# A four-layer graph kernel: the second layer's masked sums with two rounded four-byte pieces of the features over the whole array width instead of three bf16 pieces on half widths

## The chip, the core and the metric

The kernel runs on one core of a Trainium2 chip. The metric is the time that the device takes for one execution, in microseconds (us); several executions are timed and their median is compared. A profile of one more execution shows what each engine did: TensorE (PE in the rows, PEld for its weight loads), VectorE (DVE), ScalarE (ACT), GpSimd (POOL) and SyncE (SP), which only issues transfers.

## What is computed

Four layers of a graph network over 4096 nodes with 64 features each follow one another, each with a residual sum and a normalization of the rows. All take the same adjacency matrix `adj` (4096 x 4096, about 1.6% of it not zero, plus the diagonal). The change touches the second layer alone. Cut to what matters there:

```python
A = adj - diag(diag(adj))
node_support = concat([(A > 0) @ h, (A < 0) @ h], axis=1)      # 0/1 masks times features
edge_output = gru_cell(node_support, h, ...)
hw = h @ W_gat
h_plus, h_minus = (A > 0) @ hw, (A < 0) @ hw
e_plus = leaky_relu(concat([h_plus, h_minus], axis=1) @ a)
e_minus = leaky_relu(concat([h_minus, h_plus], axis=1) @ a)
att = softmax(where(A > 0, e_plus, where(A < 0, e_minus, -9e15)), axis=1)
node_output = gru_cell((att * A) @ hw, h, ...)
out = diag(adj)[:, None] * (edge_output + node_output)         # then residual and row norm
```

Two kinds of products over all nodes are needed: the 0/1 masks times `h`, and the positive and negative values of `A` times `h`.

## The kernel before

The layers run as stages of one program, and each engine has a hand-written list of instructions; semaphores alone set the order between engines. The adjacency matrix does not fit on the chip and is loaded anew in every stage, in tiles of 512 rows by 1024 columns (2 MB).

The second layer works in four quarters `q` of 1024 columns each. A quarter has sixteen steps `m`, two for each tile; a step covers two blocks of 128 rows. The loop stands once on each engine's list (lines 917, 1446 and 2096), and a count of finished steps, `pair_used`, ties them together: masks and negative parts have two buffers each, so those of step `m` may be written once TensorE has ended step `m - 2`.

In a step:
- VectorE counts the edges of the upper half for a later layer (`extend_chain`, L2093, two calls), writes the two 0/1 masks `more` and `less` in bf16 (L2122 and L2124; L2117 and L2118 where the tile holds the quarter's own diagonal, which is first read and cut out, L2106 to L2113), and last the positive part in place (L2127). That one waits for ScalarE, which reads the same tile.
- ScalarE writes the negative part (L1453) and codes of the edge counts, which it stores (L1440, L1443).
- TensorE multiplies. Features are the weights and tiles stream. L947 and L948 multiply the four-byte features with the positive and the negative part; L953 and L955 multiply the masks with the features as three bf16 pieces `parts`, whose sum is the four-byte number. Each matmul has 64 weight columns; the positive side goes to the lower half of the array's columns, the negative side to the upper half, and the two run at the same time. PSUM banks 0 and 1 collect the first kind, 2 and 3 the second.

The pieces are made ahead of the loop: ScalarE casts (`split_act`, L1228) and VectorE subtracts (`split`, L1910), alternating, for four groups of eight row blocks.

Between the steps each engine's list has the rest of the layer, worked on one or two quarters late. For the quarter before: both engines copy the sums (`copy_sums`), TensorE makes the scores (step 2), VectorE the gate (steps 3, 5), TensorE spreads the shares (step 7), VectorE weighs (8), TensorE makes the eight `hidden` blocks (steps 10 and 11, in banks 5 to 7, read by ScalarE in `read_hidden`), and VectorE the gates (13 to 15). For the quarter before that: joining, row norm, and the product with the third layer's weights (`turn_rows`, `supports`, bank 4). Behind the loop the same follows for the last quarter, while the third layer's products (`decayed`) begin in between.

Memory around it: the loads of SyncE's queue go to a ring of four tiles (L583), each when the tile that held the slot is used up; the third layer's codes and the fourth's edges take the same room later (L593 to L601, L628).

## Time and profile before

| | |
|---|---|
| median of 3 runs | 1562.92 us (1557.15 to 1565.25) |
| the profiled execution: time, span of its instructions | 1558.08 us, 1556.3 us |
| busy over the span: TensorE, VectorE, ScalarE, GpSimd | 88%, 79%, 59%, 14% |
| TensorE's granted clock over the span | 0.951 of full speed |
| the second layer's stage, first to last product of its loop | 528.8 to 977.9 us |
| products L947, L948 (records, mean of one) | 512 each, 598 ns |
| products L953, L955 (records, mean of one) | 768 each, 380 ns |

The busy share of an engine is a mean over stages with different limits, so what a change in one stage is worth has to be read in that stage. Matmuls are pipelined: a record lasts from its first to its last column, and the distance between the starts of two records tells what one costs in a stream.

### The profile page before, as it was taken

The numbers are of one execution on the slowest core, as the hardware profiler recorded it, in microseconds if no ns is written. First come the engines' busy times: TensorE is split into PE (matmuls) and PEld (weight loads), VectorE is DVE, ScalarE is ACT, GpSimd is POOL, SyncE is SP. The second block draws the span as 40 slices with busy tenths as digits, with TensorE's granted clock in tenths as the row PEclk, the third lists the DMA queues.
The fourth block names the chain that finished last, engine by engine and source line by source line (L and its number), as shares of the span: only waits on it lengthen the run. The fifth ranks groups of instructions, "written<-read, shape, count | busy, mean of one in ns | idle before, by whom it ended". The sixth has DMA issues, their size and how long they took to land. (4 is left out here: it accounts for less than half of the span.)

```text
span 1556.3 us, 20315 instructions
## 1 busy us (share of the span) xinstructions
PE 1370.9 (88%) x7818; PEld 591.1 (38%) x7818; DVE 1228.1 (79%) x1617; ACT 922.3 (59%) x888; POOL 222.0 (14%) x148
## 2 busy tenths in 40 slices
PE   5999999779977699999999999979977988888970
PEld 1433333223322444444444444534423433333430
DVE  4899866766776877876986977448697898899977
ACT  0000187348743454545555556676788899999964
POOL 1000000000000000000000000134134444444430
PEclk9999999999999699999999999999978999999995
DMA  9999599979999255553543551134723646646600
GB/s 338 409 409 409 232 400 409 413 289 394 409 414 413 109 206 213 179 183 130 183 180 126 183 180 45 55 96 151 240 92 125 199 137 209 209 136 209 215 14 27
DMA packets 135895, 348.92 MB, mean 224 GB/s; under 512 B 7732, under 2 KB 57208, under 8 KB 135544
## 3 DMA queue, kind: packets, MB, share of 16 engines
q1 hardware_dynamic: 119968, 329.27, 57.3%
q10 hardware_dynamic: 15832, 18.36, 3.3%
q8 instruction: 62, 1.02, 0.3%
q14 instruction: 33, 0.27, 0.1%
HBM read 329.78 MB, written 17.83 MB: 223 GB/s over the span
## 5 line engine op out<-in xcount | busy, mean ns | idle before, releaser
L947 PE MATMUL ps<-ring,X 128*64 128x512 f32 x512 | 264.3, 598 | 15.2 <-DVE ring L2127 15.2
L948 PE MATMUL ps<-work,X 128*64 128x512 f32 x512 | 264.3, 598 | 0.0
L1453 ACT ACTIVATE work<-ring 128x2048 f32<-128x2048 f32 x64 | 122.3, 1911 | 156.9 <-PE ps L955 123.4
L953 PE MATMUL ps<-work 128*64 128x512 bf16 x768 | 208.3, 380 | 0.0
L955 PE MATMUL ps<-work 128*64 128x512 bf16 x768 | 208.3, 380 | 0.0
L719 POOL TENSOR_TENSOR ring<-ring,work 128x1024 f32<-128x1024 f32 x72 | 171.1, 2377 | 224.8 <-DVE work L2377 224.8
L816 PE MATMUL ps<-ring,work 128*64 128x512 f32 x672 | 158.1, 615 | 22.8 <-DMA ring<-in_adjT 22.7
L705 POOL TENSOR_SCALAR work<-ring 128x1024 int16<-128x1024 uint8 x24 | 27.7, 1156 | 1008.8 <-DMA ring<-codes 933.1
L953 PEld LDWEIGHTS ps<-work 128*64 128x64 bf16 x768 | 84.8, 110 | 177.9 <-issue 152.4
L1279 ACT ACTIVATE work<-work,code_bias 128x2048 uint8<-128x2048 bf16 (+1 forms) x32 | 62.3, 1947 | 92.0 <-DVE work L1870 82.0
L1214 ACT ACTIVATE turn_in<-ps 128x512 f32<-128x512 f32 x12 | 7.2, 597 | 180.8 <-PE ps L816 180.3
L1834 DVE TENSOR_TENSOR work<-work,ring 128x1024 f32<-128x1024 f32 (+1 forms) x103 | 102.2, 992 | 9.7 <-DMA ring<-in_adjT 8.0
L2127 DVE TENSOR_SCALAR ring<-ring 128x2048 f32<-128x2048 f32 x64 | 78.1, 1220 | 39.5 <-ACT work L1453 39.5
L1079 PE MATMUL ps<-work 64*128 64x512 f32 x288 | 88.1, 691 | 17.6 <-DVE work L2390 16.0
L816 PE MATMUL ps<-ring,X 128*64 128x512 f32 x352 | 85.7, 631 | 17.2 <-DMA ring<-in_adjT 17.2
L816 PE MATMUL ps<-work 128*64 128x512 f32 x352 | 83.3, 618 | 11.1 <-DMA work<-in_adjT 11.1
L816 PEld LDWEIGHTS ps<-ring,work 128*64 128x64 f32 x672 | 45.9, 140 | 122.3 <-issue 86.6
L947 PEld LDWEIGHTS ps<-ring,X 128*64 128x64 f32 x512 | 68.7, 137 | 58.5 <-issue 16.8
L2390 DVE SCALAR_TENSOR_TENSOR work<-ps,work 128x1024 f32<-128x1024 f32 x72 | 87.4, 1214 | 1.1 <-PE ps L1090 1.1
L2122 DVE TENSOR_SCALAR work<-ring 128x2048 bf16<-128x2048 f32 x48 | 58.7, 1224 | 35.7 <-PE ps L955 35.5
L2093 DVE SCALAR_TENSOR_TENSOR stage_words<-ring,stage_words 128x512 bf16<-128x512 f32 x124 | 84.9, 684 | 0.6
L955 PEld LDWEIGHTS ps<-work 128*64 128x64 bf16 x768 | 84.8, 110 | 0.0
(366 smaller groups left out, 2768.1 us busy)
## 6 DMA issues: line engine op xcount, KB each, us to landing
ring<-in_adjT SPq DMA_DIRECT2D x88, 2048.0 KB, 16.0
work<-in_adjT SPq DMA_DIRECT2D x28, 2048.0 KB, 19.7
ring<-in_adjT SPq DMA_DIRECT2D x24, 1024.0 KB, 9.3
ring<-in_adjT SPq DMA_DIRECT2D x48, 512.0 KB, 3.6
ring<-codes SPq DMA_DIRECT2D x32, 512.0 KB, 3.7
ring<-in_adjT SPq DMA_DIRECT2D x64, 256.0 KB, 3.0
codes<-work ACTq DMA_DIRECT2D x32, 256.0 KB, 6.1
codes<-work ACTq DMA_DIRECT2D x64, 128.0 KB, 1.7
```

What stands on the lines that cost most here:

```text
L719: nc.gpsimd.tensor_tensor(u.edges, u.edges, u.angle, ALU.mult).then_inc(weighted, 1)
L816: mm = nc.tensor.matmul(ps[i * F:(i + 1) * F, a.banks + h, :], rows_of(a, k), a.room[:, k, cols], start=start, stop=stop)
L947: nc.tensor.matmul(ps[0:F, h, :], rows, ring[:, r, k, cols], start=start, stop=stop)
L948: nc.tensor.matmul(ps[F:P, h, :], rows, negs[:, pair, i, cols], start=start, stop=stop)
L953: nc.tensor.matmul(ps[0:F, 2 + h, :], part, more[:, pair, i, cols], start=start and t == 0, stop=stop and t == 2)
L955: mm = nc.tensor.matmul(ps[F:P, 2 + h, :], part, less[:, pair, i, cols], start=start and t == 0, stop=stop and t == 2)
L1079: mm = nc.tensor.matmul(ps[:, u.banks + h, :].rearrange("p (t c) -> p t c", t=2), UT[h * F:(h + 1) * F, b * P:(b + 1) * P], u.columns(node ...
L1453: nc.scalar.activation(negs[:, pair], ring[:, s % RING, 2 * pair:2 * pair + 2, :], ACT.Relu, scale=-1.0).then_inc(negs_made, 1)
L1834: ins = V.tensor_tensor(sums, sums, edges, ALU.add)
L2093: V.scalar_tensor_tensor(later1[:, (j + 1) % GB, :], edges, 0.0, later1[:, j % GB, :], ALU.not_equal, ALU.add).then_inc(later_made, 1)
L2127: V.tensor_scalar(edges, edges, 0.0, None, ALU.max).then_inc(rect_ready, 1)
L2390: V.scalar_tensor_tensor(u.angle, ps[:, u.banks:u.banks + 2, :].rearrange("p h c -> p (h c)"), 0.5 * DIST_SCALE, u.angle, ALU.max, ALU.add ...
```

## The change

The features are split in two pieces instead of three. Both pieces are numbers of the rounded four-byte format (`float32r`): ScalarE rounds the feature to it, and VectorE subtracts, which leaves the rest exactly. They stand side by side, so that one load of 128 weight columns holds both. Masks are written in the same format, two four-byte buffers each. A matmul of a mask then covers the whole array width: one piece's sums on the lower 64 partitions, the other's on the upper 64. The positive and the negative masks have banks of their own, 2 and 3 and 4 and 5. `copy_sums` adds the two pieces: ScalarE copies one half of each pair of banks, VectorE adds the other.

The masks take more room. One of them takes a slot of the ring, which is left with three; `shares` and the gate now share a buffer. With two banks more taken, the hidden blocks alternate between two banks (three in the last quarter), the row transposes and supports of the first two quarters use bank 7, and supports and hidden blocks change their steps: supports at step 10, hidden blocks at 11 and 12.

```diff
+RING1 = 3
...
+        with ExitStack() as under:
+            under.enter_context(nc.sbuf_tensor("ring_low", [P, RING1, GB, QC], F32))
+            less = under.enter_context(nc.sbuf_tensor("less", [P, 2, 2, QC], F32R))
         ring = sb("ring", [P, RING, GB, QC])
...
+            more = under.enter_context(nc.sbuf_tensor("more", [P, 2, 2, QC], F32R))
+            parts = under.enter_context(nc.sbuf_tensor("parts", [P, NB, 2 * F], F32R))
...
+        def hid_banks(n):
+            return 3 if tail_quarter(n) else 2
+        def hid_bank(n, c):
+            return 8 - hid_banks(n) + c % hid_banks(n)
+        def row_bank(n):
+            return 4 if n >= 2 else 7
...
+        def slot1(q, s):
+            return (q * NS + s + 1) % RING1
+        def used1(T):
+            return 2 + 2 * (T + 1)
...
-                        sp.wait_ge(pair_used, q * PAIRS + (2 + 2 * (s - RING + 1)))
+                        sp.wait_ge(pair_used, used1(q * NS + s - RING1))
...
-            sp.wait_ge(pair_used, 2 + 2 * (SLOTS - RING + 1))
+            sp.wait_ge(pair_used, used1(SLOTS - 3))
...
             def score(n):
                 for copied in sums_copied:
-                    pe.wait_ge(copied, 2 * (n + 1))
+                    pe.wait_ge(copied, 3 * (n + 1))
+                pe.wait_ge(hT_copied, n + 1)
...
             def hidden(n, blocks):
-                    if c >= 3:
-                        pe.wait_ge(hid_read, n * CB + c - 2)
+                    if c >= banks:
+                        pe.wait_ge(hid_read, n * CB + c - banks + 1)
+                    if c == 1 and 2 <= n + 1 < NQ:
+                        pe.wait_ge(support_read, n)
...
             def turn_rows(n):
+                if n < 2:
+                    pe.wait_ge(sums_weighted, n + 2)
...
-                    if q and m == 10:
-                        hidden(q - 1, range(4))
-                    if q >= 2 and m == 11:
+                    if q >= 2 and m == 10:
                         supports(q - 2)
                     if q and m == 11:
+                        hidden(q - 1, range(4))
+                    if q and m == 12:
                         hidden(q - 1, range(4, CB))
...
                             nc.tensor.matmul(ps[0:F, h, :], rows, ring[:, r, k, cols], start=start, stop=stop)
                             nc.tensor.matmul(ps[F:P, h, :], rows, negs[:, pair, i, cols], start=start, stop=stop)
+                    for i in range(2):
+                        k = 2 * pair + i
...
+                        for t, masks in enumerate((more, less)):
                             if start and q:
-                                pe.wait_ge(sums_copied[h], 2 * q)
-                            for t in range(3):
-                                part = parts[:, g * GB + k, t * F:(t + 1) * F]
-                                nc.tensor.matmul(ps[0:F, 2 + h, :], part, more[:, pair, i, cols],
-                                                 start=start and t == 0, stop=stop and t == 2)
-                                mm = nc.tensor.matmul(ps[F:P, 2 + h, :], part, less[:, pair, i, cols],
-                                                      start=start and t == 0, stop=stop and t == 2)
+                                pe.wait_ge(sums_copied[0], 3 * q - 1 + t)
+                            for h in range(2):
+                                cols = slice(h * HALF, (h + 1) * HALF)
+                                mm = nc.tensor.matmul(ps[:, 2 + 2 * t + h, :], parts[:, g * GB + k, :],
+                                                      masks[:, pair, i, cols], start=start, stop=stop)
                     mm.then_inc(pair_used, 1)
...
         def split_act(act):
+            for n in range(NQ):
+                blocks = slice(n * CB, (n + 1) * CB)
+                act.wait_ge(normed[0], n + 1)
+                nc.scalar.activation(parts[:, blocks, 0:F], X[:, blocks, :], ACT.Copy).then_inc(part_made[0][0], 1)
...
             def copy_sums(n):        # ScalarE
                 nc.scalar.activation(weighted_in[:, HALF:QC], ps[:, 1, :], ACT.Copy).then_inc(sums_copied[1], 1)
-                nc.scalar.activation(turn_in[:, HALF:QC], ps[:, 3, :], ACT.Copy).then_inc(sums_copied[1], 1)
+                for t in range(2):
+                    mine, other = slice(t * F, (t + 1) * F), slice((1 - t) * F, (2 - t) * F)
+                    nc.scalar.activation(turn_in[mine, :], ps[other, 2 + 2 * t:4 + 2 * t, :].rearrange(
+                        "p h c -> p (h c)"), ACT.Copy).then_inc(sums_copied[1], 1)
...
             def split():
+                for n in range(NQ):
+                    blocks = slice(n * CB, (n + 1) * CB)
+                    dve.wait_ge(part_made[0][0], n + 1)
+                    V.tensor_tensor(parts[:, blocks, F:2 * F], X[:, blocks, :], parts[:, blocks, 0:F].bitcast(F32),
+                                    ALU.subtract).then_inc(rest_made[0][0], 1)
...
             def copy_sums(n):        # VectorE
                 V.tensor_copy(weighted_in[:, 0:HALF], ps[:, 0, :]).then_inc(sums_copied[0], 1)
-                V.tensor_copy(turn_in[:, 0:HALF], ps[:, 2, :]).then_inc(sums_copied[0], 1)
+                for t in range(2):
+                    mine = slice(t * F, (t + 1) * F)
+                    dve.wait_ge(sums_copied[1], 3 * n + 2 + t)
+                    V.tensor_tensor(turn_in[mine, :], ps[mine, 2 + 2 * t:4 + 2 * t, :].rearrange("p h c -> p (h c)"),
+                                    turn_in[mine, :], ALU.add).then_inc(sums_copied[0], 1)
```

ScalarE's order of hidden blocks and supports moves by the same steps, and its first two pieces of work for the third layer (`make_decays`) go from steps 12 and 14 of the last quarter to 14 and 15.

## Rows read from the trace of the kernel before

**Rows 1.** Busy us and (instructions) of each engine by stretch, granted clock, DMA.

```profile
528.80:628.75 99.95, 99.93 (x648) 45.69 (x648) 79.29 (x94) 48.27 (x35) 0.00 (x0) 0.98 0.47 170
628.75:743.87 115.12, 114.69 (x729) 52.97 (x728) 90.63 (x123) 55.88 (x56) 0.00 (x0) 1.00 0.46 165
743.87:860.65 116.78, 116.78 (x747) 54.92 (x746) 98.42 (x137) 62.03 (x67) 0.00 (x0) 1.00 0.45 163
860.65:977.90 117.25, 116.54 (x742) 54.25 (x742) 93.24 (x129) 63.42 (x62) 2.36 (x2) 1.00 0.38 134
```

**Rows 2.** The page's groups: shapes, count, busy us, mean ns, idle before.

```profile
L947 PE MATMUL ps<-ring,X 128*64 128x512 f32 x512 | 264.3, 598 | 15.2 <-DVE ring L2127 15.2
...
L953 PE MATMUL ps<-work 128*64 128x512 bf16 x768 | 208.3, 380 | 0.0
```

**Rows 3.** Order of time, TensorE: start us, us; second quarter, steps 10 and 11.

```profile
705.19 0.59 PE L947 MATMUL ps<-ring,X 128*64 128x512 f32 x1
...
705.62 0.38 PE L953 MATMUL ps<-work 128*64 128x512 bf16 x1
...
706.05 0.38 PE L953 MATMUL ps<-work 128*64 128x512 bf16 x1
...
712.61 0.64 PE L947 MATMUL ps<-ring,X 128*64 128x512 f32 x1
```

**Rows 4.** Order of time, TensorE, in the third layer: full and half width.

```profile
985.59 1.90 PE L983 MATMUL ps<-ring,work 128*128 128x512 bf16 x8
987.42 1.05 PE L996 MATMUL ps<-ring,work 128*64 128x512 bf16 x8
988.41 1.90 PE L983 MATMUL ps<-work 128*128 128x512 bf16 x8
```

**Rows 5.** Four-byte transposes in order of time; a four-byte weight load by shape.

```profile
742.88 1.06 PE L848 MATMUL ps<-ident,X 128*64 128x128 f32 x8
...
L880 PEld LDWEIGHTS ps<-mid_w,work 65*128 65x128 f32 x64 | 10.9, 191 | 1.6 <-issue 1.6
```

**Rows 6.** Order of time, VectorE, a plain step of the first quarter.

```profile
549.56 1.23 DVE L2122 TENSOR_SCALAR work<-ring 128x2048 bf16<-128x2048 f32 x1 [1.93 <-PE ps L955]
...
552.44 1.22 DVE L2127 TENSOR_SCALAR ring<-ring 128x2048 f32<-128x2048 f32 x1
553.58 0.69 DVE L2093 SCALAR_TENSOR_TENSOR stage_words<-ring,stage_words 128x512 bf16<-128x512 f32 x1
555.58 1.23 DVE L2122 TENSOR_SCALAR work<-ring 128x2048 bf16<-128x2048 f32 x1 [1.32 <-PE ps L955]
```

**Rows 7.** Order of time, VectorE, the third quarter: its ends and turning points.

```profile
743.04 0.68 DVE L1943 COPY work<-ps 128x512 f32<-128x512 f32 x1
...
806.22 1.23 DVE L2127 TENSOR_SCALAR ring<-ring 128x2048 f32<-128x2048 f32 x1
...
818.07 1.23 DVE L2127 TENSOR_SCALAR ring<-ring 128x2048 f32<-128x2048 f32 x1 [5.83 <-ACT work L1453]
...
858.68 1.22 DVE L2127 TENSOR_SCALAR ring<-ring 128x2048 f32<-128x2048 f32 x1
```

**Rows 8.** Copies of 64 x 1024 from PSUM: ScalarE (time), VectorE (by shape).

```profile
747.64 1.03 ACT L1341 ACTIVATE work<-ps 64x1024 f32<-64x1024 f32 x1 [0.74 <-ACT work L1440]
...
L2239 DVE COPY work<-ps 64x1024 f32<-64x1024 f32 x6 | 7.4, 1227 | 0.1
```

**Rows 9.** Order of time: the split ahead of the stage, first and last.

```profile
514.82 1.15 ACT L1228 ACTIVATE work<-X 128x512 bf16<-128x512 f32 x2 [6.69 <-PE ps L833]
...
521.47 0.91 DVE L1916 MEMSET work<- 1x1024 f32 x1 [0.27 <-issue]
```

**Rows 10.** Order of time, TensorE: the scores behind the last quarter.

```profile
979.32 2.18 PE L859 MATMUL ps<-w_score,turn_in 128*128 128x2 f32 x16 [0.45 <-DVE turn_in L1944]
```

**Rows 11.** Line 583, the ring's loads: us from issue to landing.

```profile
DMA to landing us min/median/max: 8.1/8.6/28.7
```

**Rows 12.** By shape: VectorE's two-operand form over 2048 columns.

```profile
L1847 DVE SCALAR_TENSOR_TENSOR work<-ring,work 128x2048 bf16<-128x2048 f32 x22 | 50.2, 2283 | 0.0
```

106 lines of the change are left out of this document (46 added, 60 removed).

## The prediction

> **What bounds the kernel now.** I read the busy time by stretch first. The change touches one stage only, the second layer, from 528.8 to 977.9 us: four quarters of sixteen steps. In all four TensorE is busy for the whole stretch at a full clock, while VectorE is busy 79, 91, 98 and 93 us of 100 to 117 [rows 1]. So TensorE sets the end of this stage, but in the last three quarters VectorE is close behind. Then I read what a step is made of. Its records are two forms: the four-byte products of `rows` (lines 947 and 948, 512 records each) and the bf16 products of the masks (lines 953 and 955, 768 each) [rows 2]. The pairs run side by side, each on one half of the array's columns; a four-byte pair advances in 0.43 us, a bf16 pair in (706.05 - 705.62) / 2 = 0.215 us [rows 3]. 512 four-byte records over 64 steps are 8 pairs a step, 768 are 12: 8 x 0.43 + 12 x 0.215 = 6.02 us, and this is the distance between steps wherever nothing is slipped in. VectorE's share of a plain step starts when TensorE ends the step before last (549.56), ends with the rectified tile at 552.44 + 1.22 = 553.66, and the next begins only at 555.58, after a wait of 1.32 us on TensorE [rows 6]. The gates of an earlier quarter lie in that gap. In the third quarter they fill it: from the copy at 743.04 on VectorE has no idle time until 812.2, which is 5.83 us before the instruction at 818.07 [rows 7].
>
> **TensorE's part.** Removed from a step: 12 bf16 pairs, 12 x 0.215 = 2.58 us. Added: 8 matmuls (2 blocks x 2 masks x 2 halves) of 128 weight columns by 512, in the rounded format. No row shows one. Bounds: a bf16 matmul over all 128 columns advances in about 0.217 us ((1.90 - 0.38) / 7 between the eight records of line 983) [rows 4]; a four-byte product over 512 columns is two records of 0.43 us, 0.86 in all [rows 3]. I take the lower end. The four-byte product costs 0.86 / 0.215 = four times the bf16 one, which is what four products of pieces would cost (two pieces of each operand: two records, each at half rate). With one piece on either side, one of the four is left: 0.215 to 0.22. Against it stands that a four-byte transpose, one record by 128 columns, advances in (1.06 - 0.27) / 7 = 0.11 us, which is half rate too [rows 5]; a transpose has to bring the whole number through, so this need not hold for a rounded one, but it is the nearest row of the other kind and makes the first rival. The Trainium skill, page FP8 and Floating Point Precision, section TensorE Precision Notes, says that true FP32 is four passes (H*H + H*L + L*H + L*L) and that there is a reduced form which reads four bytes and truncates; by it a mask matmul is one pass. No run so far shows this form, and the bounds stay as they are.
>
> The mask matmuls now cover the whole width and stand between products on half the width. Changing over costs something: eight full-width records take 987.42 - 985.59 = 1.83 us instead of 8 x 0.217 = 1.74, and the four half-width pairs behind them 988.41 - 987.42 = 0.99 instead of 0.86, so 0.22 us for there and back [rows 4]. For four-byte weights I read it off the hidden blocks: 706.05 + 0.215 to 712.61 is 6.34 us [rows 3] for four blocks whose two 512-column and four 192-column records are 4 x (0.86 + 0.64) = 6.0. That is 0.34. I take 0.30. A step is then 3.44 + 8 x 0.217 + 0.30 = 5.48 us: 0.54 less (0.84 at most, without any price for changing over).
>
> **Who is late next.** A step of TensorE can start only after VectorE has made its tile. A plain step takes VectorE 553.58 - 549.56 + 0.69 = 4.71 us [rows 6], masks of four bytes included: the rectified tile is 2048 four-byte results in 1.22 us, the bf16 mask takes 1.23 [rows 6]. So a plain step stays TensorE's (5.48), one with gate work over 0.8 us does not.
> - First quarter, no gates: 16 x 0.54 = 8.6 us gained.
> - Third quarter: from the rectified tile of its first step (743.1) to that of its eleventh (806.22 + 1.23 = 807.45) VectorE has no idle time [rows 7]; these 64 us don't shrink. From there to the rectified tile of the next quarter's first step (858.68 + 1.22 = 859.90) it is 52.45 us [rows 7]. In the new order: step 10 (5.48), four hidden blocks (6.1, without the changeover that is now in the step), step 11 (5.48), four hidden blocks (6.1), steps 12 and 13 (10.96), after which step 14 starts at 34.1. Step 14's tile is ready before, at 33; then VectorE leads with its gates to 47 us. That gains 5.4.
> - The copies between quarters cost VectorE more: two copies of 0.6 become one of 0.6 and two additions from PSUM on 64 partitions x 1024, 1.14 each as issued (a copy of that form has 1.23) [rows 8]: +1.7. The third quarter's net is 3.7.
> - Second quarter: 8 us less VectorE work [rows 1]; from its ninth step TensorE leads, 8 x 0.54 = 4.3. Its first eight gain nothing: at the opening VectorE's additions wait for ScalarE's copies of the other half (1.03 us each [rows 8], half of that for 512 columns), so that they end 4.1 us after the quarter; queued behind them is the tile of the second step, ready 4.7 later at 8.8, where TensorE is free at 0.9 + 5.5 = 6.4. These 2.4 us eat what the steps give, and the gates fill the rest.
> - Fourth quarter: 5.2 us less VectorE work than the third [rows 1], its own-edge steps at the end; between 3.7 and 3.7 + 5.2, I take 5.0.
>
> Stage: 8.6 + 4.3 + 3.7 + 5.0 = 21.6 us.
>
> **The ends of the stage.** At its start twelve copies and eight subtractions alternate between ScalarE and VectorE, from 514.82 until the memset at 521.47, which opens VectorE's chain to the first step [rows 9]. Four copies (0.575 each) and one last subtraction (0.69) end at 517.8, the memset follows 0.3 later: 3.3 us gained. At its end, the score matmuls wait for the same copies as between quarters, now uncovered: ScalarE 0.5 + 1.0 + 1.0, then the second addition; they start 4.2 us after the last step, where the score now starts 1.4 after it (979.32 against 977.9) [rows 10]. 2.8 us lost; queued behind on TensorE are the first products of the third layer, and on VectorE the gates of the third and fourth quarter.
>
> Edits at nothing: the hidden blocks have two banks, not three; TensorE makes a block in 1.5 us [rows 3], and ScalarE, which reads 1024 columns in 1.03 [rows 8], reads its 512 within one block (were it a block late, 1.5 us each time). The supports move a step ahead of the hidden blocks, into the stretch that VectorE leads (1.6 us of TensorE, twice, where not covered). Three ring slots, not four: a tile is asked for when the third before it is used up, about 15 us ahead, and lands in 8.6 [rows 11]; were that cover gone, a tile late by 1 us costs 32. The code loads and room waits move by one tile of about 11 us, earlier than their use after the stage. The extra waits on the second parts and weighted sums are met a step before.
>
> **Sum.** 21.6 + 3.3 - 2.8 = 22.1 us. The profiled execution took 1558.1: 1536. The median of the runs is 4.8 higher, 1562.9, which would give 1540.8. I say 1538. Without the price of changing over the stage gains some 31 and the time is 1527; with gates biting harder, 1550.
>
> **Rivals.**
> - *Half rate* (slower): the rounded operand still streams at half rate, as in the transposes [rows 5]. Eight times 0.43: a step is 3.44 + 3.44 + 0.30 = 7.18, above VectorE everywhere; 64 x 1.16 = 74 us more, 1632. It decides from 0.28 us a matmul on, where a step is 3.44 + 2.24 + 0.30 = 6.0 and nothing is left. For it: both four-byte forms seen stream at that rate. Against: the factor four.
> - *Weight loads uncovered* (slower): each of the eight matmuls loads 128 four-byte columns. Such a load is recorded with 191 ns at line 880 [rows 5], and there 0.43 us of streaming hides it. If a stream of 0.217 hides none of, say, 0.145, a step is 6.64: 1558 + 64 x 0.62 = 1598. Against: full-width bf16 loads are hidden [rows 4]. The Trainium skill, page TensorE: Matmul & The Clock Gate, section Weight-path perf modes, says that the fast weight load is not for FP32; by its figure for a plain load, 128 / 1.2 = 107 ns (an estimate from that page), a step would be 6.3 and the time some 1578.
> - *Masks written at one result a cycle* (slower): if the rounded output costs VectorE its fast mode, a mask takes 2.28, as the 2048-wide two-operand form does [rows 12], not 1.22. VectorE's step is 6.7, its quarters some 13 us longer: about 1608. Against: four-byte output at 1.22 [rows 6].
> - *Eaten up*: full rate, but changeovers, copies and gates leave under 8 us: 1550 to 1563.
>
> **How the numbers follow.** Forecast 0.74 (own range 1520 to 1553), half rate 0.12, uncovered loads 0.04, slow masks 0.03, eaten up 0.07. Leaving out the three slower ones (0.19) gives 1518 to 1568. A measurement of this kernel tells about 0.5%, 8 us, from no change: faster 0.74, same 0.08, slower 0.18.
>
> **What would show it.** Right: mask records that advance by 0.217, changeovers of 0.2 to 0.35 in every step, first-quarter steps of 5.4 to 5.6, and VectorE as the releaser of the first products in quarters two to four. Wrong: mask records 0.43 apart (half rate); 0.3 to 0.36 apart (loads); masks of 2.2 us on VectorE; TensorE waiting for a tile's DMA; or quarters two to four that shrink as the first does, which would mean that I overrate VectorE.

## The result, and the profile after

The median falls from 1562.92 us (1557.15 to 1566.31, five runs) to 1549.79 us (1547.01 to 1551.97, five runs); the ratio is 0.9935 with a 95% interval of 0.9914 to 0.9957. So the change makes the kernel faster, by 10 us (the ratio) to 13 us (the medians) and not by the 25 that I forecast. The profiled execution took 1548.29 us (span 1546.5) where that of before took 1558.08: 9.8 us, to be compared with the 22.1 of my sum.

Busy time by quarter of the stage, columns as in [rows 1], which it answers:

```profile
525.75:619.17 93.42, 93.42 (x393) 41.40 (x393) 79.09 (x93) 48.21 (x35) 0.00 (x0) 0.97 0.53 182
619.17:733.23 114.06, 108.38 (x473) 53.48 (x473) 92.61 (x124) 58.49 (x58) 0.00 (x0) 0.99 0.48 167
733.23:848.83 115.60, 109.08 (x491) 55.27 (x491) 100.33 (x138) 64.41 (x68) 0.00 (x0) 1.00 0.47 164
848.83:964.06 115.23, 108.41 (x486) 54.87 (x487) 95.64 (x130) 64.84 (x62) 2.69 (x2) 1.00 0.42 150
```

TensorE's busy time fell by 6.5, 6.3, 7.7 and 8.1 us. The first quarter gives all of it back as time. In the others TensorE now idles 5.7, 6.5 and 6.8 us, where it was busy for (nearly) the whole stretch before, and the quarters shrink by only 1.1, 1.2 and 2.0. What ends that idle time is in the groups from 525 to 1000 us (columns as in [rows 2]):

```profile
L986 PE MATMUL ps<-ring,X 128*64 128x512 f32 x512 | 237.6, 607 | 28.7 <-DVE ring L2165 26.9 <-DVE work L1975 1.7
...
L997 PE MATMUL ps<-more,parts 128*128 128x512 f32 x256 | 86.7, 420 | 0.0
L997 PE MATMUL ps<-less,parts 128*128 128x512 f32 x256 | 79.5, 392 | 0.0
```

L2165 is VectorE's rectified tile, the last of its work in a step. Of the 28.7 us, 10.8 lie ahead of the stage's first product; of the 15.2 us in [rows 2] it was 14.0. Within the loop the idle time before these products rose from 1.1 to 17.9 us. Now one step of TensorE in order of time (start, length), which answers [rows 3]:

```profile
548.21 0.59 PE L986 MATMUL ps<-ring,X 128*64 128x512 f32 x1
...
548.74 0.73 PE L997 MATMUL ps<-more,parts 128*128 128x512 f32 x2
549.31 0.62 PE L997 MATMUL ps<-less,parts 128*128 128x512 f32 x2
549.77 0.62 PE L997 MATMUL ps<-more,parts 128*128 128x512 f32 x2
550.23 0.62 PE L997 MATMUL ps<-less,parts 128*128 128x512 f32 x2
550.77 0.64 PE L986 MATMUL ps<-ring,X 128*64 128x512 f32 x1
```

Two mask matmuls advance in 0.46 us: 0.23 each, full rate (a bf16 matmul of this width takes 0.217 [rows 4]). From the last four-byte pair (548.21 + 0.43) to the next step's first (550.77) it is 2.13 us; less 8 x 0.23 that leaves 0.29 around the masks, and some 0.05 more within the first four-byte pair: 0.34 for changing over. The first quarter's steps take 5.62 us (before 6.02, forecast 5.48).

### The profile page after: what moved, and what is told of

It is laid out like the page before. It is cut to its first block and busy times, and to the rows that moved or that the text cites. A ratio compares the mean times of both kernels' runs of the same rounds, so it can differ in the third digit from the quotient of the medians.

```text
span 1546.5 us, 18239 instructions
## 1 busy us (share of the span) xinstructions
PE 1338.4 (87%) x6769; PEld 588.3 (38%) x6794; DVE 1233.3 (80%) x1617; ACT 925.8 (60%) x884; POOL 222.6 (14%) x148
## 5 line engine op out<-in xcount | busy, mean ns | idle before, releaser
L986 PE MATMUL ps<-ring,X 128*64 128x512 f32 x512 | 237.6, 607 | 28.7 <-DVE ring L2165 26.9
L987 PE MATMUL ps<-work,X 128*64 128x512 f32 x512 | 237.7, 608 | 0.0
L739 POOL TENSOR_SCALAR work<-ring 128x1024 int16<-128x1024 uint8 x24 | 27.7, 1157 | 1010.7 <-DMA ring<-codes 936.7
L2165 DVE TENSOR_SCALAR ring<-ring 128x2048 f32<-128x2048 f32 x64 | 78.2, 1222 | 37.1 <-ACT work L1491 37.1
L850 PE MATMUL ps<-ring,X 128*64 128x512 f32 x352 | 87.1, 641 | 17.4 <-DMA ring<-in_adjT 17.4
L850 PE MATMUL ps<-work 128*64 128x512 f32 x352 | 81.7, 608 | 10.8 <-DMA work<-in_adjT 10.8
L997 PE MATMUL ps<-more,parts 128*128 128x512 f32 x256 | 86.7, 420 | 0.0
L1477 ACT ACTIVATE work<-stage_words,code_bias 128x1024 uint8<-128x1024 bf16 (+1 forms) x64 | 71.1, 1111 | 15.8 <-DVE stage_words L2131 15.8
L997 PE MATMUL ps<-less,parts 128*128 128x512 f32 x256 | 79.5, 392 | 0.0
L1908 DVE SCALAR_TENSOR_TENSOR work<-ring,work 128x512 bf16<-128x512 f32 x85 | 58.5, 689 | 23.8 <-DMA ring<-in_adjT 19.1
L1638 ACT ACTIVATE work<-work 128x1024 f32<-128x1024 f32 x72 | 75.4, 1047 | 1.7 <-DVE work L2428 0.5
```

Source lines behind the costliest of these rows:

```text
L850: mm = nc.tensor.matmul(ps[i * F:(i + 1) * F, a.banks + h, :], rows_of(a, k), a.room[:, k, cols], start=start, stop=stop)
L986: nc.tensor.matmul(ps[0:F, h, :], rows, ring[:, r, k, cols], start=start, stop=stop)
L987: nc.tensor.matmul(ps[F:P, h, :], rows, negs[:, pair, i, cols], start=start, stop=stop)
L997: mm = nc.tensor.matmul(ps[:, 2 + 2 * t + h, :], parts[:, g * GB + k, :], masks[:, pair, i, cols], start=start, stop=stop)
L1638: nc.scalar.activation(v.angle, v.angle, ACT.Ln, scale=2.0 / DIST_SCALE).then_inc(angle_made, 1)
L2165: V.tensor_scalar(edges, edges, 0.0, None, ALU.max).then_inc(rect_ready, 1)
```

## The experiments

The theory: TensorE's saving is real, but behind the first quarter VectorE leads, and what is left is eaten at the openings and in the tail by the added work of joining the pieces. The rivals: the mask products or the changeovers cost more than they seem; ScalarE or the waits lead, not VectorE. The lengths below are from the first product of a quarter to that of the next, the last to its last product. Steps are counted from 0, and a step "comes after" so many us, counted between its first product and that of the step before. "Own-edge" steps are the four of a quarter whose tiles hold its own diagonal.

| kernel | quarters, us | ratio to before, 95% |
|---|---|---|
| before | 99.9, 115.1, 116.8, 117.2 | |
| after | 93.4, 114.1, 115.6, 115.2 | 0.9935 (0.9914 to 0.9957) |
| 1 two changeovers | 98.1, 115.6, 118.3, 118.5 | 1.0012 (0.9992 to 1.0033) |
| 2 short counts, after | 93.1, 108.0, 110.8, 110.8 | 0.9830 (0.9794 to 0.9865) |
| 3 short counts, before | 100.5, 114.5, 116.8, 116.1 | 0.9992 (0.9968 to 1.0017) |
| 4 plain copies | 92.9, 111.3, 113.3, 113.0 | 0.9863 (0.9822 to 0.9905) |
| 5 alternating order | 91.1, 113.1, 115.6, 116.2 | 0.9945 (0.9924 to 0.9966) |
| 6 half the tile on ScalarE | 92.6, 114.9, 118.9, 115.2 | 0.9975 (0.9962 to 0.9987) |
| 7 whole tile on ScalarE | 93.8, 114.1, 122.4, 117.9 | 1.0001 (0.9987 to 1.0015) |
| 8 plain four-byte masks | 173.8, 186.9, 189.7, 189.0 | one run, 1849.9 us |
| 9 counts on GpSimd | 122.2, 133.2, 139.5, 138.0 | 1.0572 (1.0540 to 1.0604) |
| 10 early copies | 89.5, 112.0, 114.7, 113.8 | 0.9874 (0.9854 to 0.9895) |
| 11 early copies, counts on GpSimd | 122.1, 132.8, 139.0, 136.8 | 1.0539 (1.0513 to 1.0564) |
| 12 early copies, short counts | 90.5, 105.4, 107.7, 108.0 | 0.9742 (0.9685 to 0.9800) |

### 1. What a changeover costs

```diff
-                    for i in range(2):
-                        k = 2 * pair + i
-                        start = m == 0 and i == 0
-                        stop = m == PAIRS - 1 and i == 1
```

(The mask loop moves into the loop over blocks.)

> The changed kernel with its products in another order: in each step the mask matmuls of a block follow that block's four-byte products, so the array changes over from half to full width and back twice a step, not once. Everything else is as it was. The question is what a changeover costs, the term I forecast with 0.30 us. Theory: the changed kernel's step of 5.62 us in the first quarter is 3.44 (four-byte products) + 1.84 (masks) + one changeover of 0.34, so a second one gives 5.96 us; the time then rises by 16 x 0.34 in the first quarter and by what of the other quarters TensorE leads (some 17 steps, 5.8 us), 8 to 12 us, 1558 to 1562. By my forecast's term the step would be 5.92. Rival: the changeover is cheap (0.1 us) and the 0.14 us that a step is over my forecast comes once a step from something else (the wait for the tile, the mask records themselves): step 5.72, the time up by 2 to 4.

One step in order of time, its two blocks one behind the other:

```profile
554.18 0.64 PE L986 MATMUL ps<-ring,X 128*64 128x512 f32 x1
...
556.05 0.73 PE L993 MATMUL ps<-more,parts 128*128 128x512 f32 x2
...
557.17 0.64 PE L986 MATMUL ps<-ring,X 128*64 128x512 f32 x1
...
560.17 0.64 PE L986 MATMUL ps<-ring,X 128*64 128x512 f32 x1
```

A step of the first quarter takes 5.99 us, so a second change there and back costs 0.37 us. The time is 1563.07 us, 0.8% over after, as the theory has it: the stage grows by 12.2 us, not by 64 x 0.37 = 23.7, because VectorE hides the rest. The rival (0.1 us) is out. My term of 0.30, read from bf16 and from the hidden blocks, was too small by 0.04 (what a step of after leaves for it) to 0.07.

### 2 and 3. VectorE relieved, after and before

```diff
-                V.scalar_tensor_tensor(later1[:, (j + 1) % GB, :], edges, 0.0, later1[:, j % GB, :], ALU.not_equal,
-                                       ALU.add).then_inc(later_made, 1)
+                V.scalar_tensor_tensor(later1[:, (j + 1) % GB, 0:F], edges[:, 0:F], 0.0, later1[:, j % GB, 0:F],
+                                       ALU.not_equal, ALU.add).then_inc(later_made, 1)
```

> The changed kernel with VectorE's work made smaller: the edge counts for a later layer (two instructions a step) are made over 64 columns, not 512, the other columns are zero. That part of the result is left out; TensorE's work is untouched. Each step costs VectorE about 1.0 us less. Theory: the gain in quarters two to four was lost because VectorE leads the first ten steps of each. Then these quarters fall from 114.1, 115.6 and 115.2 us to near TensorE's own busy time of 108.4 to 109.1 plus 1 to 2 us for the opening, first products wait for VectorE at the openings only, and the time falls by 12 to 17 us, to 1533 to 1538. The first quarter stays at 93.4. Rival: VectorE is only the last to report, and TensorE's extra pieces (changeovers, hidden blocks, supports, lower clock) make the quarters long: the time falls by less than 4 us.

> The control for the same edit: the kernel before with the edge counts over 64 columns (that part of the result is left out). Theory: TensorE leads it nearly everywhere (busy 115 to 117 us of each of quarters two to four), so the same relief brings 0 to 3 us, 1560 to 1563. The difference between this and the changed kernel with the same edit is then what the change saves on TensorE when VectorE is out of the way: some 24 us. Rival: the relief helps both alike (10 us or more), and VectorE says nothing about why the change gained less than forecast.

After with the short counts, by quarter:

```profile
525.01:618.09 93.08, 93.08 (x392) 41.34 (x393) 64.66 (x93) 48.21 (x35) 0.00 (x0) 0.98 0.52 182
618.09:726.10 108.01, 106.53 (x473) 53.04 (x473) 78.37 (x123) 57.46 (x57) 0.00 (x0) 1.00 0.50 175
726.10:836.91 110.81, 108.76 (x491) 55.23 (x491) 86.58 (x137) 63.60 (x68) 0.00 (x0) 1.00 0.49 171
836.91:947.70 110.79, 108.16 (x486) 54.81 (x487) 82.41 (x130) 64.95 (x63) 2.36 (x2) 1.00 0.45 157
```

VectorE has 14 us less in each, and quarters two to four lose 6.1, 4.8 and 4.4 us; TensorE's idle time falls from 5.7, 6.5 and 6.8 to 1.5, 2.1 and 2.6. The same relief brings the kernel before 0.1%, which is nothing. Between the two with short counts lie 0.9992 - 0.9830 = 1.6%, 25 us (some 7 us either way by the two intervals), and their quarters add up to 25.1 us less: this is what the change is worth on TensorE when VectorE is mostly out of the way, 0.40 us for each of 64 steps. It is close to my forecast of 24.9 for a kernel in which VectorE is in the way. This pair decides for the theory.

### 4. Without the additions

```diff
-                    nc.scalar.activation(turn_in[mine, :], ps[other, 2 + 2 * t:4 + 2 * t, :].rearrange(
-                        "p h c -> p (h c)"), ACT.Copy).then_inc(sums_copied[1], 1)
+                nc.scalar.activation(turn_in[:, HALF:QC], ps[:, 3, :], ACT.Copy).then_inc(sums_copied[1], 2)
...
-                    V.tensor_tensor(turn_in[mine, :], ps[mine, 2 + 2 * t:4 + 2 * t, :].rearrange("p h c -> p (h c)"),
-                                    turn_in[mine, :], ALU.add).then_inc(sums_copied[0], 1)
+                V.tensor_copy(turn_in[:, 0:HALF], ps[:, 2, :]).then_inc(sums_copied[0], 2)
```

(The first mask products of a quarter also wait for both engines' copies.)

> The changed kernel with the sums copied between quarters as in the kernel before: one copy of 128 x 512 for the mask sums on each engine, no additions of the two pieces (the addition is left out, so the sums that go on are not the right ones). Theory: the two additions on VectorE (2.48 us, behind ScalarE's two copies of 1.03) cost 1.9 us at each of the three openings and hold the scores in the tail; while TensorE waits its clock falls, which costs once more (1.7 us in the second quarter near 660 us, 1.4 us on the scores in the tail). Without them the second quarter's step 1 comes after 6.0 to 6.5 us and not 8.10, its records keep the full clock, the scores start 1.5 us after the last product and not 4.24 and take 2.2 us and not 3.58; in all 8 to 12 us less, 1538 to 1542. Rival: the wait only moves, since gates and masks queue on VectorE anyway: less than 4 us, and the low clock in the second quarter stays.

0.7% less than after (11 us). The second quarter's step 1 comes after 5.63 us (8.10 in after), quarters two to four lose 2.8, 2.3 and 2.2 us, and the scores start 2.27 us after the last product and take 2.20. They did not start at 1.5: the change also makes them wait for `copy_h` (L1376 in this run's row), which ScalarE makes behind its copies.

```profile
957.73 2.20 PE L894 MATMUL ps<-w_score,turn_in 128*128 128x2 f32 x16 [1.40 <-ACT work L1376]
```

One part went the rival's way: the low clock near the second quarter's step 6 stayed. Step 6 still comes after 8.00 us, and its first products then advance in 0.85 to 0.91 us, not 0.43:

```profile
655.78 1.12 PE L986 MATMUL ps<-ring,X 128*64 128x512 f32 x1 [2.31 <-DVE ring L2159]
...
656.69 1.06 PE L986 MATMUL ps<-ring,X 128*64 128x512 f32 x1
...
657.54 1.06 PE L986 MATMUL ps<-ring,X 128*64 128x512 f32 x1
```

So that idle time is not the additions'. It is gone in experiment 2 (step 6 after 5.62), thus VectorE's: in after, steps 4 to 7 of the second quarter hold the own-edge work, and between the masks of two such steps VectorE has no pause. In order of time, VectorE:

```profile
642.14 1.23 DVE L2155 TENSOR_SCALAR more<-ring 128x2048 fp32r<-128x2048 f32 x1
...
648.07 1.23 DVE L2155 TENSOR_SCALAR more<-ring 128x2048 fp32r<-128x2048 f32 x1
...
656.08 1.23 DVE L2155 TENSOR_SCALAR more<-ring 128x2048 fp32r<-128x2048 f32 x1
...
662.00 1.23 DVE L2155 TENSOR_SCALAR more<-ring 128x2048 fp32r<-128x2048 f32 x1
```

An own-edge step costs it 5.93 us, just under the old step of 6.02 and over the new one of 5.62; with the share gate in it, 8.01. My sum went by the "plain step" of 4.71 and spoke of own-edge steps in the fourth quarter only, without their length.

### 5. Half the changeovers

```diff
+                    for part in (by_masks, four_byte) if m % 2 else (four_byte, by_masks):
+                        mm = part()
```

> The changed kernel with the order of products alternating: even steps four-byte products first and masks last, as before, odd steps masks first and four-byte products last. Two neighbouring steps then share a width, so there is one changeover there and back in two steps instead of two. Every product and every wait is kept. From the run with two changeovers a step (5.99 against 5.62 us a step) one there and back costs 0.37 us. Theory: two steps of the first quarter take 11.24 - 0.37 = 10.87 us; the first quarter falls by 3.0 us, the other quarters by 0.18 for each of some 17 steps that TensorE leads: 5 to 6 us in all, 1543 to 1546. Where VectorE leads (first ten steps of quarters three and four) nothing changes. Rival: the price lies not in the change of width but in the start of a step or of a row of four-byte products after anything else; then steps stay at 5.62 and the time at 1549.

Two steps of the first quarter take 10.87 us, to the hundredth, and that quarter loses 2.4 us. But quarters two to four together gain nothing (344.9 us both times), where I had expected 3.1, and the ratio is that of after. TensorE's steps got cheaper by another 0.19 us, and VectorE took most of it: the second quarter loses 1.0 us and the third nothing. The fourth is 1.0 us longer, and that is TensorE's clock in this one profile: its last step follows a wait of 2.09 us, runs for 3.4 us at a granted clock of 0.50 and takes 7.25 us, not 5.70.

```profile
956.39 0.76 PE L1000 MATMUL ps<-more,parts 128*128 128x512 f32 x2 [2.09 <-DVE ring L2171]
```

Without that the three quarters would have gained some 1.6 us. In experiment 10, which has the same order, the same wait of 2.09 us leaves the clock at 1.00.

### 6 and 7. The rectified tile on ScalarE

```diff
-                    V.tensor_scalar(edges, edges, 0.0, None, ALU.max).then_inc(rect_ready, 1)
+                    V.tensor_scalar(edges[:, 0, :], edges[:, 0, :], 0.0, None, ALU.max).then_inc(rect_ready, 1)
...
+                    nc.scalar.activation(other, other, ACT.Relu).then_inc(rect_act, 1)
```

(Experiment 7: both blocks on ScalarE.)

> The changed kernel with the rectified tile of the second block of each step made by ScalarE and not by VectorE (in place, after VectorE's masks and ScalarE's own negative part); all results are kept. VectorE's step is shorter by 1.14 - 0.57 = 0.57 us less some 0.1 for a wait on its own masks, ScalarE's longer by about 1.0. Theory (VectorE leads): a step with the own-edge work falls from 5.93 on VectorE to some 5.4, under TensorE's 5.62, so that the second quarter's step 6 comes after 7.3 and not 8.01 and its records keep the full clock; the first ten steps of quarters three and four lose 0.4 us each: 8 us less in all, 1540 to 1544. Rival: ScalarE is late with its half, because its queue holds codes, copies and hidden blocks: no gain, 1548 or more.

> The changed kernel with the whole rectified tile made by ScalarE; all results are kept. VectorE's step is shorter by 1.14 us, about what the shorter edge counts took from it (1.0 us, 15 us of time), ScalarE's longer by 1.8: 1.8 + 1.1 + 1.8 = 4.7 of TensorE's 5.62, and 7 us more a quarter for copies, exponentials and hidden blocks. Theory: if VectorE's load alone made quarters two to four long, they fall to 109 to 112 us as with the short counts, the time to 1535 to 1540. Rival: the tile is then ready 0.7 us later behind the masks (1.9 us against 1.2) and ScalarE's queue holds it up at the openings: quarters two to four fall by less than 2 us each and ScalarE is named as the releaser of TensorE's first products.

Both go the rival's way: 0.4% and 0.7% over after. ScalarE has spare time (58 to 65 us busy of 115), but its list is in order, and codes, copies and exponentials that wait for others stand ahead of the tile. The waits name it; the first row is of experiment 6, the second of 7 (us in total, times, longest; the longest is the one ahead of the stage's first product):

```profile
PE ps L989 <- ACT ring L1501: 27.7, 12, 12.0
```

```profile
PE ps L987 <- ACT ring L1499: 37.1, 15, 12.8
```

In the third quarter of experiment 7 the first two steps come after 9.4 and 9.6 us (7.4 and 7.3 in after), steps 3 to 6 after 5.62 to 5.65: relief in the middle, a dearer opening. These two don't speak against VectorE as the one that leads; they show that its work can't be moved for nothing.

### 8. The plain four-byte format

```diff
-                                mm = nc.tensor.matmul(ps[:, 2 + 2 * t + h, :], parts[:, g * GB + k, :],
-                                                      masks[:, pair, i, cols], start=start, stop=stop)
+                                mm = nc.tensor.matmul(ps[:, 2 + 2 * t + h, :], parts[:, g * GB + k, :].bitcast(F32),
+                                                      masks[:, pair, i, cols].bitcast(F32), start=start, stop=stop)
```

> The changed kernel with the mask products in the plain four-byte format: the same bits in masks and pieces, the same full width and order, only the format that the instruction names is another. It tests my argument that the plain format makes four products of pieces and the rounded one makes one. Theory: each product is two records at half rate, 0.43 us each, 0.86 us for 512 columns against 0.23; a step takes 3.44 + 8 x 0.86 + 0.35 = 10.7 us, so that TensorE leads everywhere, and the stage grows by about 64 x 5.05 = 323 us less the 15 to 20 us in which TensorE waits now: 1850 to 1860. Rival: the rounded format owes its rate to the masks and pieces having few bits, and the plain one is as fast: 1550.

```profile
561.69 1.98 PE L997 MATMUL ps<-more,parts 128*128 128x512 f32 x4
563.51 1.88 PE L997 MATMUL ps<-less,parts 128*128 128x512 f32 x4
```

The same bits take twice the records (1024 of L997 over the stage, 512 in after), and four advance in 1.72 to 1.82 us: two of 0.43 for a matmul, 0.86, against one of 0.23. A step takes 10.65 us, the execution 1849.9. The factor of four on which I bet against the half-rate rival is the factor that separates the two formats. The Trainium skill, page FP8 and Floating Point Precision, section TensorE Precision Notes, has four passes for true FP32; the trace agrees, with 0.86 against 0.23 us, 3.7 times.

### 9 and 11. The counts on GpSimd

```diff
+                    nc.gpsimd.tensor_scalar(marks[:], ring[:, r, 2 * pair:2 * pair + 2, HALF:QC], 0.0, 0.0,
+                                            ALU.is_equal, ALU.is_equal).then_inc(marked, 1)
...
+                nc.gpsimd.tensor_tensor(later1[:, (j + 1) % GB, :], marks[:, j % 2, :], later1[:, j % GB, :],
+                                        ALU.add).then_inc(later_made, 1)
```

> The changed kernel with the edge counts for a later layer made by GpSimd, which is idle in this stage, and not by VectorE; all results are kept. GpSimd marks the two blocks' edges (one instruction of 128 x 1024) and adds twice (128 x 512). From its rows of the changed kernel (1.16 us for a one-operand 128 x 1024, 2.38 us for a two-operand 128 x 1024) that is some 3.6 us a step, less than TensorE's 5.62. VectorE's step is shorter by two instructions, 1.2 us. Theory (VectorE leads quarters two to four): as with the short counts, the quarters fall to 108 to 111 us and the time by 12 to 17 us, 1533 to 1538. Rival: two engines that read the same tiles slow each other down, so that VectorE's masks take longer than 1.22 us or GpSimd longer than a step and VectorE's rectified tile, which waits for the counts, comes late: 1548 or more.

> The edits of the counts on GpSimd and of the early copies together; all results are kept. Theory: with VectorE out of the way TensorE leads nearly everywhere, and then the alternating order, which brought nothing alone, is worth its 0.18 us a step: quarters of 91, 105 to 107, 107 to 109 and 107 to 109 us, the tail as in the run before; in all 15 (VectorE) + 8 (order, quarters two to four) + 5 (tail) less than the changed kernel: 1519 to 1527. Rival: VectorE leads again at 5.44 us a step, since a step with the own-edge work still costs it 4.7 us and gates come on top: 1530 to 1536.

The rival, and by far: 100 us slower than after. Groups of experiment 9 from 525 to 1050 us, GpSimd, then VectorE (count, busy us, mean ns):

```profile
L758 POOL TENSOR_SCALAR work<-ring 128x1024 bf16<-128x1024 f32 x63 | 295.0, 4683 | 10.1 <-POOL stage_words L746 9.9 <-ACT work L1508 0.2
L746 POOL TENSOR_TENSOR stage_words<-work,stage_words 128x512 bf16<-128x512 bf16 x124 | 190.4, 1535 | 30.3 <-DVE stage_words L2152 11.4 <-ACT work L1508 5.9
```

```profile
L2177 DVE TENSOR_SCALAR more<-ring 128x2048 fp32r<-128x2048 f32 x48 | 84.7, 1766 | 7.8 <-PE ps L1026 7.4
```

GpSimd needs 4.68 us for what I had estimated at 1.16 from its row in another stage, 7.8 us a step in all, and the same mask takes VectorE 1.77 instead of 1.22. My estimate had two faults. The row of 1.16 reads one-byte and writes two-byte numbers (L739, in the third layer); in this form, from four bytes to bf16, no instruction of experiment 9 takes less than 3.63 us, and one of these has VectorE at work for 1.25 us of it only. And the two engines do slow each other: GpSimd's addition takes 1.15 us where VectorE is idle and up to 2.09 where it is not. The lines by source (shortest, median, longest in ns):

```profile
L758 POOL TENSOR_SCALAR work<-ring x64: 3627/4586/5392, 518.8 to 1041.0; 128x1024 bf16<-128x1024 f32 x64
L746 POOL TENSOR_TENSOR stage_words<-work,stage_words x124: 1150/1242/2087, 523.9 to 1046.2; 128x512 bf16<-128x512 bf16 x124
```

How much of the 4.68 us is the form and how much the neighbour, no run here separates. The Trainium skill, page SBUF — State Buffer, section Who interferes with whom, says that the two share a pair of ports, that in VectorE's two-port modes the first to issue holds it for its whole instruction while the other blocks, and that VectorE's `tensor_scalar` can be of that kind; the rows agree in that both lose, and no run here shows the ports. Experiment 11 (0.3% less than 9) could not show what it was meant for.

### 10 and 12. Early copies

```diff
+                        if m == PAIRS - 1:
+                            mm.then_inc(masks_summed, 1)
...
-                act.wait_ge(pair_used, (n + 1) * PAIRS + 2)
+                act.wait_ge(masks_summed, n + 1)
...
                 nc.scalar.activation(stats[:, 4, blocks], stats[:, 3, blocks], ACT.Sqrt).then_inc(roots_taken, 1)
+                if n < 2:
+                    act.preload_act_table_set("exp_and_others")
```

(On top of the order of experiment 5. In the tail VectorE adds first and copies bank 0 last.)

> The changed kernel with three edits to its waits, all results kept: the order of products alternates (odd steps masks first), so that the mask sums of a quarter are complete some 3.7 us before its last product; their copies and additions wait for those alone (in the tail VectorE makes the additions before it copies bank 0); and ScalarE loads the table of its next functions right behind the square roots, not ahead of the first hidden block. VectorE's load is not touched. Theory: the alternating order alone brought nothing, since VectorE leads; the tail is another matter, there VectorE is idle. The scores start 1.0 to 1.5 us after the last product and not 4.4, and take 2.2 us and not 3.6, since TensorE is not idle long enough to lose its clock: 4 to 5 us; the step behind the first hidden blocks comes after 11.7 and not 12.5 us in quarters three and four where TensorE leads: up to 1.7. In all 1542 to 1546. Rival: what the tail gains is lost again at the third layer's first products, which wait for something else: 1548 to 1551.

> The early copies (with the alternating order) and the short counts together: what the run with the counts on GpSimd was to show and could not, because the two engines slowed each other. The counts over 64 columns leave out part of the result. Theory: TensorE's saving is worth nothing while VectorE leads and its full size when VectorE is out of the way. The alternating order alone brought quarters two to four together 0 us; with the short counts quarters of 89 to 91, 105 to 106, 107.5 to 109 and 107.5 to 109 us follow, 2 to 3 us less each than the 108.0, 110.8 and 110.6 of the short counts without it, and the time is 1539 - 15 - 6 to 8, 1516 to 1519. Rival: the order costs what it saves (waits for the mask buffers, which odd steps release in another order), so that quarters two to four stay at 108 to 111 us: 1523 to 1525.

Experiment 10 beats both kernels: 1539.19 us, 0.9874 of before, 0.6% or some 9.5 us under after (expected 1542 to 1546, which left the first quarter out). The scores start 2.86 us after the last product, not 1.0 to 1.5, because ScalarE is still at work for the third layer when the mask sums are complete; but they take 1.95 us, and the third layer's first eight products, which come next, 1.89 us (3.32 in the kernel before, where the granted clock was 0.60 from 981.5 to 985 us). Whether these 3 us reach the end, a single profile can't tell: from the stage's last product to the end it is 581.6 us, 582.4 in after.

```profile
959.99 1.95 PE L895 MATMUL ps<-w_score,turn_in 128*128 128x2 f32 x16 [1.85 <-DVE work L1989]
961.80 1.89 PE L1034 MATMUL ps<-work 128*128 128x512 bf16 x8
```

The step behind the first hidden blocks comes after 11.46 us in quarters three and four (12.29 in experiment 5 with the same order). Of the gain over after 3.9 us lie in the first quarter: 2.7 are the order's (as in experiment 5, less its first step), and the other 1.2 are the first step's length, which differs from kernel to kernel (6.9 to 9.0 us, experiment 8 aside) without an edit that bears on it.

Experiment 12 gives what experiment 11 was to give: 1517.15 us, within the 1516 to 1519 expected. The same edits that take 2.0, 0.9 and 1.4 us from quarters two to four when VectorE leads (experiment 10 against after) take 2.6, 3.1 and 2.8 us from them once VectorE is relieved (12 against 2): 4.3 and 8.5 us. Not all of this is the order's. 1.6 and 3.3 us lie in the opening step, which the early copies shorten, 2.1 both times in the step of the first hidden blocks, and 0.6 and 3.1 in all others, where the order acts. This is a second sign for the theory, beside experiments 2 and 3; the order alone with the short counts was not run.

## Why the prediction was right or wrong

The direction, the full rate and the time's range were right; the size was not, and the time of 1549.8 lies where my forecast and the rival "eaten up" meet. That rival's mechanism is the one that acted, and 0.07 was too little for it. The range was 33 us wide, so that the time fell into it says little for the sum: every quarter of the stage gained less than I wrote.

| term | forecast | measured |
|---|---|---|
| start of the stage | +3.3 | 528.82 - 525.75 = +3.1 |
| first quarter | +8.6 | +6.5 |
| second | +4.3 | +1.1 |
| third | +3.7 | +1.2 |
| fourth | +5.0 | +2.0 |
| tail | -2.8 | 9.8 - 13.8 = -4.0 |
| sum | 22.1 | 9.8 |

**The step of TensorE.** Mask matmul 0.23 for 0.217, changeover 0.34 for 0.30 (0.37 by experiments 1 and 5): 3.44 + 8 x 0.23 + 0.34 = 5.62, not 5.48. That is 2.2 us in the first quarter and 0.14 for each step that TensorE still leads later. The matmul lies near the end that I took. For changing over I went between two rows (0.22 in bf16, 0.34 in four bytes), where the second was the nearer one, and the measured price lies at it or just over it. *Half rate*, *uncovered loads* and *slow masks* are out: 0.23 a matmul, and 1.22 us a mask on VectorE. With uncovered loads at the figure that the Trainium skill, page TensorE: Matmul & The Clock Gate, section LDWEIGHTS (loading the stationary operand), has for a plain load, my estimate of a step was 6.3 us; the measured 5.62 shows no load of that size uncovered. (In *slow masks* VectorE's step is 4.71 + 2 x 1.05 = 6.8 us, not 6.7.)

**Who is late next: the step that failed.** 13.0 us forecast for quarters two to four, 4.3 measured: 8.7 of the 12.3 us that are missing. The opening was right (additions end 4.2 us after the quarter, forecast 4.1; the second tile is ready after 8.9, forecast 8.8). Wrong was the assumption that in and behind a stretch which VectorE leads nothing more is lost and TensorE gets its full saving. VectorE's step is not 4.71 us everywhere: own-edge steps take it 5.93, more than TensorE's new 5.62.
- Second quarter, first eight steps: I wrote 0, it is -2.2 (55.2 us from the first step's start to the ninth's, before 53.0); the other eight gave 3.2 of 4.3, 8 x 0.14 less. The own-edge steps (5.93 on VectorE) and the gate fall behind; TensorE idles 2.32 us, and then its clock falls, which costs once more. TensorE, in order of time, then the stretch with its granted clock (columns as in [rows 1]):

```profile
659.63 0.64 PE L986 MATMUL ps<-ring,X 128*64 128x512 f32 x1 [2.32 <-DVE ring L2165]
...
660.54 1.00 PE L986 MATMUL ps<-ring,X 128*64 128x512 f32 x1
...
661.34 1.06 PE L986 MATMUL ps<-ring,X 128*64 128x512 f32 x1
...
663.89 0.65 PE L986 MATMUL ps<-ring,X 128*64 128x512 f32 x1
```

```profile
660.60:664.00 3.40, 3.40 (x12) 0.95 (x10) 3.26 (x5) 2.02 (x2) 0.00 (x0) 0.50 1.00 379
```

  Four pairs take 3.35 us instead of 1.71: the lower of the two levels, 1.2 GHz. No term of mine had this. The length of the wait alone does not decide it: at the opening of the same quarter TensorE idles longer, and the clock stays at 1.00.

```profile
627.27 0.64 PE L986 MATMUL ps<-ring,X 128*64 128x512 f32 x1 [2.40 <-DVE ring L2165]
```

```profile
627.27:631.00 3.73, 3.73 (x17) 1.20 (x18) 3.73 (x5) 1.49 (x2) 0.00 (x0) 1.00 0.13 38
```

- Third quarter: the stretch that VectorE leads grew by 2.3 us (forecast 1.7), and what follows gained 3.4 of 5.4, read between the ends of three rectified tiles as in [rows 7]. Of the 2.0 missing, 0.7 are five steps at 0.14, 0.9 the hidden blocks, and the rest the supports, which run ahead of step 10 and push it 1.3 us behind its tile.

```profile
731.26 1.22 DVE L2165 TENSOR_SCALAR ring<-ring 128x2048 f32<-128x2048 f32 x1
...
797.85 1.22 DVE L2165 TENSOR_SCALAR ring<-ring 128x2048 f32<-128x2048 f32 x1
...
846.86 1.22 DVE L2165 TENSOR_SCALAR ring<-ring 128x2048 f32<-128x2048 f32 x1
```

- Fourth quarter: 5.0 was a choice between 3.7 and 8.9, and 2.0 came. Its first eight steps take 0.6 us longer than before, the other eight 2.6 less: there the late hidden block costs 0.85, and ahead of the last step TensorE idles 1.98 us for the tile of an own-edge step.
- The hidden blocks on two banks were one of my edits at nothing ("TensorE makes a block in 1.5 us, ScalarE reads it within one block"). The first block does come late: ScalarE, behind square roots, loads a table first; with three banks that was covered (the step behind the first four blocks came after 12.42 us in the third quarter of the kernel before and 12.37 in its second). ScalarE's row, then TensorE's:

```profile
807.65 1.28 ACT L1394 ACT_TABLE_LOAD   x1 [3.08 <-PE ps L921]
```

```profile
809.66 1.13 PE L917 MATMUL ps<-mid_w,work 65*128 65x512 f32 x2 [0.57 <-ACT work L1395]
```

  I had priced a late block at 1.5 us each time; it is 0.85, twice (12.52 against 11.67 us in the second quarter). With the table loaded earlier (experiment 10) it is below 0.1.

**The tail.** The start of the scores was forecast 4.2 us after the last step and is 4.24. What I left out is the clock: TensorE idles 3.37 us before them, its granted clock is then 0.50, and they take 3.58 us where [rows 10] have 2.18.

```profile
963.90 1.04 PE L882 MATMUL ps<-ident,X 128*64 128x128 f32 x8
968.30 3.58 PE L894 MATMUL ps<-w_score,turn_in 128*128 128x2 f32 x16 [3.37 <-DVE turn_in L1979]
```

2.8 + 1.4 = 4.2, and this is what is missing at the first hidden blocks behind them: they come 9.6 us earlier than before, where the stage ended 13.8 earlier.

**What I said would show it.** Right signs came: changeovers of 0.34 to 0.37 (I had named 0.2 to 0.35), VectorE as releaser in quarters two to four, nothing of SyncE's loads. The steps of 5.62 lie just over the 5.4 to 5.6 named. What stays open: behind the stage, single profiles of much the same code differ by up to 9 us (578.2 us in experiment 12, 587.2 in experiment 2). So the tail's 4 us, as a difference of two ends, could be chance; the 4.2 us up to the first hidden blocks are read from rows. Open, too, is why TensorE's clock fell after some waits and not after others of the same length.

## What to carry to other kernels

When two engines are close, cost a saving on the first only up to the next-longest step of the second, and look for that step among all of its kinds (here four own-edge steps of 5.93 us in sixteen), not at its plain one; then relieve the second engine in both kernels, for that prices the change by itself. Give each idle stretch that a change opens on TensorE a chance of a second price, the clock behind it (here 1.6 us, and not each time). An engine that is idle isn't free: ScalarE's list was in the wrong order for the tile, and GpSimd slowed VectorE down. And price an instruction from a row with its own number formats.

## What the runs showed of the hardware

- The rounded four-byte format streams 512 columns through all 128 weight columns in 0.23 us; the plain one takes 0.86 for the same bits.
- Changing between half and full width costs 0.34 to 0.37 us there and back with four-byte operands (experiments 1 and 5 and the step of after; 0.22 in the bf16 products of [rows 4]). The Trainium skill, page TensorEngine Tiling (Array Packing), section Key Properties, says that a change of mode drains the array; it gives no time.
- After 2.32 us without work TensorE's granted clock was 0.50 for some 3.4 us and its records took twice as long; after 2.40 us and 1.98 us in the same trace it stayed at 1.00. After 2.09 us it fell in experiment 5 and not in experiment 10.
- VectorE writes the rounded format as fast as bf16: 1.22 us for 2048 columns.
- A GpSimd addition over 128 x 512 in bf16 took 1.15 us with VectorE idle and up to 2.09 beside it; VectorE's masks took 1.77 us in the mean there, instead of 1.22.
